# Attention scores as three fp32r products; the remainders of queries, keys and shared weights taken by GpSimd

## The reference

```
q = (queries @ Wq + bq).reshape(B, L, 16, 16)      # L = 512
k = (keys @ Wk + bk).reshape(B, S, 16, 16)         # S = 64
v = (values @ Wv + bv).reshape(B, S, 16, 16)
scores = einsum('blhd,bshd->bhls', q, k)           # fp32
scores = where(causal, -inf, scores)
attn = softmax(scores * 0.25)
out = einsum('bhls,bshd->blhd', attn, v).reshape(B, L, 256) @ Wo + bo
```

## Time and profile before

| | |
|---|---|
| median of 3 runs | 917.37 us (916.71 to 919.8) |
| profiled execution | 916.98 us |
| its span | 915.3 us |
| PE busy | 886.2 us (97%) |
| PEld | 778.9 us (85%) |
| DVE | 625.2 us (68%) |
| ACT | 524.0 us (57%) |
| POOL | 331.0 us (36%) |

### The profile page before, as it was taken

The page is one execution under the profiler, slowest core; times in us unless marked ns, Lnnn a source line. Parts: engine busy times, 40 slices in busy tenths (PEclk is TensorE's granted clock), DMA queues, the critical chain, the costliest instruction groups (busy, mean ns, idle before and its releaser), DMA issues.

```text
span 915.3 us, 20404 instructions
## 1 busy us (share of the span) xinstructions
PE 886.2 (97%) x6734; PEld 778.9 (85%) x6743; DVE 625.2 (68%) x1465; ACT 524.0 (57%) x1050; POOL 331.0 (36%) x318
## 2 busy tenths in 40 slices
PE   8999998999998999999999999999999999999996
PEld 6688995566554888888988999999999999999996
DVE  5998696899877776666656766575665657575553
ACT  4683434556455655446444775575766667575552
POOL 3477222211302555555553224232232323322222
PEclk9999999999999999999999999999999999999998
DMA  9300020000002111111226556335353533533332
GB/s 251 121 1 1 2 92 1 2 1 1 1 7 94 51 54 67 66 61 67 84 95 224 141 114 145 47 54 128 48 131 47 139 47 47 139 47 47 47 47 35
DMA packets 87855, 64.00 MB, mean 70 GB/s; under 512 B 58112, under 2 KB 80832, under 8 KB 87680
## 3 DMA queue, kind: packets, MB, share of 16 engines
q0 software_dynamic: 17504, 34.87, 16.5%
q1 hardware_dynamic: 60192, 26.80, 11.5%
q10 hardware_dynamic: 10112, 1.70, 1.1%
HBM read 38.58 MB, written 24.77 MB: 69 GB/s over the span
## 4 chain that ended last, share of the span: by engine, by line
PE 79%; DVE 7%; DMA 4%; ACT 4%; issue 4%; POOL 1%; SPq 0%; ACTq 0%; DVEq 0%; POOLq 0%
PE PS L137 22%; PE PS L139 21%; PE PS L138 21%; DMA metar<-routed_rows 3%; PE PS L894 3%; PE PS L309 2%; PE PS L924 2%; PE PS L938 1%; PE PS L944 1%; ACT hideh L1913 1%; DVE mxpad L1138 1%; PE PS L1402 1%; ACT act32e L1915 1%; PE PS L1384 1%; DMA win<-in_W_inT 1%
## 5 line engine op out<-in xcount | busy, mean ns | idle before, releaser
L1944 POOL DMA_INDIRECT out_rows<-y,toki x70 | 113.5, 1622 | 265.9 <-DVE y L1974 246.6
L1913 ACT ACTIVATE hideh<-PS,be 128x256 fp32r<-128x256 f32 x280 | 143.7, 513 | 101.3 <-PE PS L139 101.2
L143 DVE TENSOR_TENSOR hidel<-act32e,hideh 128x256 fp32r<-128x256 f32 x280 | 118.0, 425 | 84.0 <-ACT act32e L1915 81.6
L137 PE MATMUL PS<-xTeh,wfch 128*128 128x256 f32 x560 | 158.6, 283 | 1.9 <-ACT act32e L1915 1.1
L137 PE MATMUL PS<-wprh,hideh 128*128 128x256 f32 x560 | 158.5, 283 | 1.9 <-DVE hidel L143 1.9
L138 PE MATMUL PS<-xTel,wfch 128*128 128x256 f32 x560 | 157.6, 281 | 0.0
L139 PE MATMUL PS<-xTeh,wfcl 128*128 128x256 f32 x560 | 157.5, 281 | 0.0
L139 PE MATMUL PS<-wprh,hidel 128*128 128x256 f32 x560 | 156.5, 279 | 0.0
L138 PE MATMUL PS<-wprl,hideh 128*128 128x256 f32 x560 | 156.3, 279 | 0.0
L1915 ACT ACTIVATE act32e<-PS,be 128x256 f32<-128x256 f32 x280 | 144.6, 516 | 8.7 <-DVE hidel L143 8.1
L137 PEld LDWEIGHTS PS<-wprh,hideh 128*128 128x128 f32 x560 | 104.9, 187 | 5.2 <-DVE hidel L143 4.9
(11 more groups left out here) (273 smaller groups left out, 2059.8 us busy)
## 6 DMA issues: line engine op xcount, KB each, us to landing
xb<-routed_rows SPq DMA_DIRECT2D x144, 64.0 KB
fcraw<-in_Wfc POOLq DMA_DIRECT2D x8, 1024.0 KB, 6.0
prraw<-in_Wproj POOLq DMA_DIRECT2D x8, 1024.0 KB, 9.0
out_rows<-X SPq DMA_DIRECT2D x8, 512.0 KB, 2.9
X<-in_x SPq DMA_DIRECT2D x7, 512.0 KB, 7.6
routed_rows<-pads SPq DMA_DIRECT2D x8, 272.0 KB, 4.3
out_rows<-y,toki POOLq DMA_INDIRECT x70, 3.8
ctx<-in_ctxT SPq DMA_DIRECT2D x4, 256.0 KB, 7.1
```

What stands on the lines that cost most here:

```text
L137: nc.tensor.matmul(out, wh, xh, start=first, stop=False)
L143: return eng.tensor_tensor(out, whole, high.bitcast(F32), ALU.subtract)
L1913: nc.scalar.activation(hid[0][:, j, :], PS[:, j % 4, 0:BLK], ACT.Gelu_apprx_tanh, bias=bias)
L1944: nc.gpsimd.indirect_dma_start(out=out, out_offset=bass.IndirectOffsetOnAxis(ap=toki[:, h:h + 1], axis=0), in_=y[:, h, :], in_offset=None, ...
```

## The change

Queries and keys are split into high and low fp32r parts, and each score is three fp32r products (`PARTS`) in the place of one fp32 product.

- The query is written by ACT twice, once rounded (`qT[0]`) and once whole into a single buffer `q32`; GpSimd subtracts (`q_low`) into `qT[1]`. ACT writes the second whole query only when GpSimd has read the first, and it is GpSimd that now raises `qT_ready`.
- The keys of a block are copied (rounded) and subtracted by GpSimd (`split_keys`) into one of two pairs `kpair`. For b of 2 and over it waits for the key scores of block b-2.
- The remainders of the shared expert's weights move from DVE to GpSimd (`weight_low`).
- DVE normalises the four tiles of the block three ahead in two parts: the first two at the end of the round as before, the last two in the next round, behind the maxima of tile 0.

```
-            qT = old("qT", [P, 2, KD, L])
+            qT = [old("qTh", [P, 2, KD, L], F32R), Place(w_at)("qTl", [P, 2, KD, L], F32R)]
+            q32 = Place(yD_at + 3 * pair_bytes)("q32", [P, L])
+            kpair = [[Place(at)("kpair%d%s" % (par, n), [P, KD, HG * S], F32R) ...
+            PARTS = ((0, 0), (0, 1), (1, 0))
...
# row_scores
+                    pe.wait_ge(k_split, 2 * b + 2)
                     for m in range(KD):
-                        for half in range(2):
-                            last = nc.tensor.matmul(at, qT[rows, b % 2, m, t * P:(t + 1) * P],
-                                kbd[rows, b, m, :].rearrange("p (i n) -> p i n", i=2), ...
+                        for n, (qp, kp) in enumerate(PARTS):
+                            for half in range(2):
+                                last = nc.tensor.matmul(at, qT[qp][rows, b % 2, m, t * P:(t + 1) * P],
+                                    kpair[b % 2][kp][rows, m, :].rearrange("p (i n) -> p i n", i=2), ...
...
# key_scores
-                    for j in range(NG):
-                        nc.tensor.matmul(PS[:, j, :], kbd[rows, b, m, ...], qT[rows, b % 2, m, :], ...
+                    for n, (qp, kp) in enumerate(PARTS):
+                        for j in range(NG):
+                            nc.tensor.matmul(PS[:, j, :], kpair[b % 2][kp][rows, m, ...], qT[qp][rows, b % 2, m, :], ...
...
# evac_q, on ACT
-                    nc.scalar.activation(qT[:, b % 2, m, :], PS[...], ACT.Identity, bias=...).then_inc(qT_ready, 1)
+                    nc.scalar.activation(qT[0][:, b % 2, m, :], PS[...], ACT.Identity, bias=...)
+                    if b + m:
+                        act.wait_ge(qT_ready, KD * b + m)
+                    nc.scalar.activation(q32[:], PS[...], ACT.Identity, bias=...).then_inc(q_high, 1)
...
# on GpSimd
+                def split_keys(b):
+                    if b >= 2:
+                        pool_wait(pool, s_psum, 2 * NG * (b - 1))
+                    kh, kl = kpair[b % 2]
+                    nc.gpsimd.tensor_copy(kh[:], kbd[:, b]).then_inc(k_split, 1)
+                    pool_wait(pool, k_split, 2 * b + 1)
+                    low(nc.gpsimd, kl[:], kbd[:, b], kh[:]).then_inc(k_split, 1)
+                def q_low(b):
+                    for m in range(KD):
+                        pool_wait(pool, q_high, KD * b + m + 1)
+                        low(nc.gpsimd, qT[1][:, b % 2, m, :], q32[:], qT[0][:, b % 2, m, :]).then_inc(qT_ready, 1)
...
                 pool_wait(pool, bo_ready, 1)
+                split_keys(0)
+                q_low(0)
+                split_keys(1)
                 add_bo(0)
                 for b in range(1, B):
                     if b + 1 < B:
                         rstds(b + 1)
+                    q_low(b)
+                    if b + 1 < B:
+                        split_keys(b + 1)
                     add_bo(b)
+                    if b < 5:
+                        weight_low(b - 1)
...
# on DVE, round b
                     maxima(b + 1, 0)
+                    if behind and after:
+                        for t in pair(1):
+                            apply_part(b + 2, t)
...
-                    if 0 < b < 5:
-                        low(nc.vector, parts[1][:, part], whole[:, part], parts[0][:, part]).then_inc(ws_low, 1)
...
                     if b + 3 < B:
-                        for t in range(TB):
+                        for t in pair(0):
                             apply_part(b + 3, t)
```

More of the change, by code:

```diff
@@ L165, in build @@
         ident16 = ab("ident16", [P, P], BF16)
+        yD_at = ab.at
         yD = ab("yD", [P, KE * L])
@@ L890, in row_scores @@
                     for m in range(KD):
-                        for half in range(2):
[L892 to L899, removed]
+                        for n, (qp, kp) in enumerate(PARTS):
+                            for half in range(2):
+                                rows = slice(half * P // 2, (half + 1) * P // 2)
+                                at = PS[:, 4 + half, :].rearrange("p (i m n) -> p i m n", i=2, m=KD)[:, :, m, :]
+                                end = m == KD - 1 and n == len(PARTS) - 1
+                                last = nc.tensor.matmul(
+                                    at, qT[qp][rows, b % 2, m, t * P:(t + 1) * P],
+                                    kpair[b % 2][kp][rows, m, :].rearrange("p (i n) -> p i n", i=2),
+                                    start=m + n == 0, stop=t > 0 and end, skip_group_check=True)
+                                if t and end:
+                                    last.then_inc(n_psum, 1)
                     if t == 0:
@@ L1011, in evac_q @@
                     act.wait_ge(q_psum, KD * b + m + 1)
-                    nc.scalar.activation(qT[:, b % 2, m, :], PS[:, q_bank(b, m), :], ACT.Identity,
-                                         bias=bq[:, m:m + 1]).then_inc(qT_ready, 1)
+                    nc.scalar.activation(qT[0][:, b % 2, m, :], PS[:, q_bank(b, m), :], ACT.Identity,
+                                         bias=bq[:, m:m + 1])
+                    if b + m:
+                        act.wait_ge(qT_ready, KD * b + m)
+                    nc.scalar.activation(q32[:], PS[:, q_bank(b, m), :], ACT.Identity,
+                                         bias=bq[:, m:m + 1]).then_inc(q_high, 1)
                 def exps(b, m):
@@ L1098, in add_bo, with weight_low @@
                         nc.gpsimd.tensor_tensor(xs, xs, bo[:], ALU.add).then_inc(bo_added, 1)
+                def split_keys(b):
[9 more added lines that the diff above has]
+                        low(nc.gpsimd, qT[1][:, b % 2, m, :], q32[:], qT[0][:, b % 2, m, :]).then_inc(qT_ready, 1)
+                def weight_low(i):
+                    pool_wait(pool, ws_high, i + 1)
+                    parts, whole = ((wfs, fcraw), (wps, prraw))[i // 2]
+                    part = slice(i % 2 * (whole.shape[1] // 2), (i % 2 + 1) * (whole.shape[1] // 2))
+                    low(nc.gpsimd, parts[1][:, part], whole[:, part], parts[0][:, part]).then_inc(ws_low, 1)
                 first[3](pool)
```

21 lines of the change are left out of this document (13 added, 8 removed).

## The result

| | before | after |
|---|---|---|
| median, 20 runs each | 917.02 us (913.97 to 920.24) | 920.8 us (918.9 to 925.45) |
| profiled execution's span | 915.3 us | 920.3 us |
| mean granted clock in it | 0.991 | 0.988 |

The ratio is 1.0048, 95% interval 1.0033 to 1.0062: slower by about 4.4 us, outside what can be taken for no change; the two medians are 3.8 apart. The forecast was 920.8, 3.45 above the first median of the kernel before (917.37). Whether its steps were right is another question, and the answer is: most of them, with three that were not.

The account below looks back on a forecast made before the run. TensorE was taken as the bound (79% of the chain), DVE a second bound close behind. Eight steps summed to +3.45 us on 916.98, giving 920.4, or 920.8 on the median's scale; range 913 to 926.5.

Parts of the forecast that it names:

- Step 1: Attention start: GpSimd splits block 0's keys before its queries, row scores 1.6 late, some made up; +1.1 us (0.5 to 2).
- Step 2: Block 1's second query, before block 0's key scores: ACT and GpSimd in turn, 4.8 us; +2.8 us (2.3 to 4).
- Step 3: After TensorE idles about 3.6 us before block 0's key scores: half clock for 3.4 us; +1.5 us (0 to 1.7).
- Steps 4 and 5: Block 0's round: cheaper products, -0.8 us; its end, with no output projection between, the query late in full, +1.0 us.
- Step 6: Four rounds, walked point by point, at -0.05 us each, plus 0.4 back from a bo-addition collision; -0.6 us.
- The lock: In rounds, GpSimd and DVE wait for each other's whole instruction; without it a round would be 0.9 us shorter.
- Step 7: The round without normalisation at its end: DVE has slack; -0.55 us.
- Step 8: The last round and key scores 7, partly behind DVE; -1.0 us.
- A: Rival: remainders come in time, rounds give 0.9 us rather than 0.05; 914.5 us, chance 0.25.
- B: Rival: TensorE's idle in a round grows past 1.7 us, where the clock falls; 926.5 us, chance 0.10.
- C: Rival: weight loads lie open under 256-column passes, 1.4 us per row-score group for 1.06; 937 us, chance 0.03.
- D: Rival: time unchanged, since waits on DVE stand in the same places; 917.4 us, chance with its neighbourhood 0.15.

Follow-up runs that it names:

- Experiment 4: Changed kernel with a second buffer for the whole query; one run, transposed maxima to key scores 6.29 us for 7.06, rounds 19.30 to 19.32.
- experiment 3: Changed kernel with GpSimd's query subtraction replaced by one fill of 0.53 us; one run, rounds 18.39 us against 19.30.
- experiment 5: Changed kernel with 14 unused products filling TensorE's wait before block 0's key scores; ratio to the kernel before 1.002.
- filled kernels: Kernel before and changed kernel, each with unused products in two TensorE waits so the clock stays whole; attention stage 173.3 and 176.3 us.
- experiments 2: Changed kernel with GpSimd's query subtraction replaced by two fills, 1.2 us together; one run, rounds 18.83 us against 19.30.
- experiment 7: Changed kernel with query remainders taken by DVE straight from PSUM and ACT writing each query once; ratio to the kernel before 0.9997.
- experiments 6 and 11: 6: changed kernel, waits before block 0's key scores and first logits filled, 1.0022. 11: kernel before, idle times at 73 and 285 us filled, 0.9978.
- experiment 8: Changed kernel remade: DVE query remainders from PSUM, earlier key splits, wo's remainder moved, both TensorE waits filled; 910.44 us, ratio to the kernel before 0.9937.

## Why the prediction was right, and where it was not

- **Step 1, start, +1.1:** right, 1.58 late and 0.57 made up. PE waits 1.50 us there, until GpSimd's second remainder has ended; with one short fill in the place of the remainder the first row scores are back at 8.59.
- **Step 2, second query chain, +2.8:** right, 2.82. Experiment 4 shows that 0.8 of it is the single buffer. With an operation of 0.53 us in the place of the remainder (experiment 3) the stretch is 5.54 for 7.06, so 1.5 of the 2.8 goes with the remainders' length, and what stays is in ACT's second write, the short operation itself and the hand-overs.
- **Step 3, clock, +1.5 (at most 1.7):** the mechanism was right and is shown by experiment 5; the size was off. The half clock lasted 6.8 us, twice the row it was priced from, and cost 2.07.
- **Steps 4 and 5, -0.8 + 1.0:** their sum, +0.2, was right (0.19 by the filled kernels).
- **Step 6, four rounds, -0.6:** the collision went as foreseen (19.62 is gone), but a round is 0.05 longer instead of 0.05 shorter: -0.19. The walk was right within 0.11 at each of its points (above). What it had wrong lies behind them: it counted 0.2 for the second key scores, and 0.04 arrives, as the third row scores then wait for the maxima.
- **The lock:** experiments 2 and 3 show it, as 0.47 a round. The forecast laid the lost gain to the lock and the lateness together, and that is right. That without the lock the round would be 0.9 shorter is not borne out: with two fills it is 18.83, 0.42 under the kernel before, and the maxima come at Z+6.7, not 6.3 (though even a fill holds `hn` somewhat). And one link is wrong: GpSimd's second remainder does not wait for the division. It starts 0.9 us behind its last work, released by ACT's second whole query, which ends at Z+3.48; with fills, which start as late, this stays. By chance the lock would have ended at nearly the same time. The rule that the prediction drew on, the Trainium skill (SBUF — State Buffer, Who interferes with whom), has the one wait for the other's whole instruction; the trace agrees for `hn` behind a remainder, two tiles in 1.70 us for 0.72. That DVE's one-input work is held too, the rows ahead of the prediction do not show; the line of the kernel before at 127.82 (experiment 7) does, four tiles in 3.07 us for 1.38.
- **Step 7, -0.55:** right, -0.50.
- **Step 8, last round, -1.0:** wrong. By the filled kernels it gives 0.26; the last key scores wait for DVE's `mxT` (0.59 us) and the logits behind them for its xT0 remainder, so shorter products have nothing to bring there. In the profile even this was lost: the half clock behind the logits lasted 10 us for 3.4.
- **What the total owes to chance.** With the clock held the change costs 3.1 us in the stage and not 1.95, by steps 6 and 8, which were 1.15 too good together. The clock's share would be 1.3 (4.4 from the ratio less 3.1), near the 1.5; this rests on single profiles, and the medians of the filled kernels of experiments 6 and 11 (1.0022 and 0.9978, of different sessions) are 4.0 apart, with intervals that allow for 1.6 to 6.4. So the forecast of 3.45 was about 1 us short of the 4.4. That 920.8 was hit to the tenth is luck: the median of the kernel before came out 0.35 below the one that was added to, and the medians are 0.6 less apart than the ratio says.
- **The rivals.** A needed remainders in time; its condition is experiment 3, and rounds of 18.39, about the 0.85 less that it was priced at, and 910.9 us in one run. B needed waits above 1.7 us in the rounds; the longest is 0.97, before the first row scores behind round 0. Its limit of 1.7 is no limit either: the clock fell behind 1.65 and stayed behind 1.9 (last section). C is out by the pitch of 0.12, and no run shows a load of 0.11 in the open. The Trainium skill's rule (TensorE: Matmul & The Clock Gate, The mechanism) has two halves, and the one by which loads overlap only for other rows is not borne out here, as loads for the same rows are hidden; this agrees with the half on the background buffer, which no run here shows by itself. D is outside the interval.

So the products brought 0.6 us a round on TensorE (0.86 with short fills) and that was turned into waits for the two engines that make their operands; the rest of the slowdown is paid once, before the first key scores, and by the clock behind that wait.

## What to carry to other kernels

When a product is made cheaper by splitting operands, walk from the moment the operand leaves PSUM to its first use, and count each writer: here one write became write, write, wait, subtract, and DVE could do the same straight from PSUM in one operation. Before moving work to an idle GpSimd, look at what DVE does at that moment, down to copies of 64 elements: an idle engine that shares a lock is not free. And price a new wait of TensorE with the clock behind it, then see whether harmless products can stand in it; they must not wait for what the idle time waits for.

## What was not expected of the hardware

- The half clock's length is not fixed. In these profiles it is 3.4, 6.8 or 10.2 us. After the idle 3.69 it was 6.8; after 2.89 (experiment 4) 3.4; after the 1.9 us before the logits 10.2, 6.8, 3.4 or nothing, by the profile.
- Nor does the same idle time always bring it. At 73 us both kernels idle 1.93 us for the same residual. Before, the clock falls, and after, it does not:

```profile
73.30:76.70 3.40, 3.40 (x16) 3.40 (x17) 3.40 (x4) 0.50 (x1) 3.40 (x5) 0.51 0.02 5
```

```profile
72.90:76.30 3.40, 3.40 (x29) 3.40 (x30) 3.40 (x4) 0.43 (x1) 3.40 (x5) 1.00 0.02 5
```

  After an idle 1.65 in experiment 7 it fell, after 1.06 in experiment 8 it stayed. This makes much of the spread between runs of one kernel: of the changed one, the runs with a mean clock of 0.988 or less have 921.0 to 925.5 us, those at 0.993 and above 918.9 to 921.2. It also means that one profile does not price a fall for the medians.
- GpSimd's subtraction of 512 elements with two inputs took 1.26 us alone and 1.33 beside DVE, the conversion of 512 took 0.61 alone and 1.86 behind DVE's `gl`.
- DVE's one operation on PSUM with a bias and a second input (512 elements) took 0.71 to 0.75, hardly more than a plain subtraction of that size (0.68), also beside GpSimd's bo additions (two in 1.41, in experiment 8), where `hn` was held.
